# Block-causal self attention on Trainium2: the row maxima are turned one step earlier and their units are dealt out again

## What is computed

```python
scores = jnp.einsum('bhqd,bhkd->bhqk', q, kh) / jnp.sqrt(jnp.float32(D))
scores = jnp.where(allowed_pos[None, None], scores, NEG)
scores = jnp.where(causal[None, None], -jnp.inf, scores)
p = jax.nn.softmax(scores, axis=-1)
out = jnp.einsum('bhqk,bhkd->bhqd', p, vh)
```

## Time and profile before

| what | value |
|---|---|
| median of 3 runs (lowest to highest) | 3237.11 us (3233.18 to 3238.16) |
| the profiled execution's own time | 3233.07 us |
| its span | 3231.4 us |
| busy over the span: TensorE, VectorE, ScalarE, GpSimd | 93%, 55%, 38%, 60% |
| self attention's first score, last sum | 535.0 us, 1153.6 us |

### The profile page before, as it was taken

How to read it: one execution, slowest core, us unless ns; L and a number is a source line. 1 busy time by engine, 2 the same in 40 slices (tenths; PEclk the granted TensorE clock), 3 DMA queues, 4 the chain that set the end, 5 groups by cost and what they waited for, 6 DMA issues and landing times. The chain is left out here.

```text
span 3231.4 us, 39692 instructions
## 1 busy us (share of the span) xinstructions
PE 2997.9 (93%) x15242; PEld 1968.5 (61%) x15242; DVE 1766.7 (55%) x2884; ACT 1225.6 (38%) x2307; POOL 1923.7 (60%) x999
## 2 busy tenths in 40 slices
PE   7999999999999959859999999999959999999999
PEld 6888886444444438734444444444427888888887
DVE  4455657777777547647777777777532222122220
ACT  2212223555555522205666666666632111111111
POOL 3324323888887766526888888888877443333332
PEclk9999999999999979968999999999979999999999
DMA  6555764445555045453424242332042010010100
GB/s 205 173 163 189 233 206 122 109 106 115 118 117 119 17 146 195 170 137 65 87 57 99 57 94 65 72 87 57 11 134 62 27 39 30 23 40 27 40 13 14
DMA packets 199538, 310.17 MB, mean 96 GB/s; under 512 B 15011, under 2 KB 93363, under 8 KB 199347
## 3 DMA queue, kind: packets, MB, share of 16 engines
q1 hardware_dynamic: 199350, 307.64, 34.8%
HBM read 189.04 MB, written 117.44 MB: 95 GB/s over the span
## 5 line engine op out<-in xcount | busy, mean ns | idle before, releaser
L1254 POOL TENSOR_TENSOR e_probs<-e_probs 128x2048 f32<-128x2048 f32 x160 | 731.4, 4579 | 189.1 <-ACT e_probs L1230 184.3
L1230 ACT ACTIVATE e_probs<-e_st 128x512 f32<-128x512 f32 x1024 | 557.4, 598 | 407.8 <-PE e_st L1412 389.9
L1308 DVE TENSOR_REDUCE e_neg_max<-e_nat 128x1 f32<-128x1024 f32 x512 | 602.0, 1217 | 169.3 <-PE e_nat L1395 164.4
L1230 ACT ACTIVATE b_probs<-b_st 128x512 f32<-128x512 f32 (+3 forms) x768 | 340.3, 490 | 279.0 <-PE b_st L1412 268.8
L1305 DVE CUSTOM_DVE_ANT_0 b_nat<-b_nat,mask_qk 128x128 f32<-128x128 f32 (+7 forms) x512 | 374.4, 785 | 80.9 <-PE b_nat L1395 79.5
L1412 PE MATMUL e_st<-e_qs,e_ks 98*128 98x512 f32 x1024 | 395.3, 430 | 10.0 <-DMA e_qs<-e_max_lo 6.8
L1715 POOL TENSOR_TENSOR m_hid_lo<-m_hid,m_hid_hi 128x512 fp32r<-128x512 f32 x128 | 168.3, 1315 | 390.5 <-DVE m_hid_hi L1752 390.5
L1254 POOL TENSOR_TENSOR b_probs<-b_probs 128x1536 f32<-128x1536 f32 (+3 forms) x128 | 374.7, 2927 | 38.1 <-PE b_pv L1424 35.2
L1395 PE MATMUL e_nat<-e_ks,e_qs 96*128 96x512 f32 x1024 | 345.8, 422 | 40.1 <-DMA e_vs<-cv 25.4
L1752 DVE CAST m_hid_hi<-m_hid 128x512 fp32r<-128x512 f32 x128 | 58.5, 457 | 570.6 <-ACT m_hid L1631 570.6
L1412 PEld LDWEIGHTS e_st<-e_qs,e_ks 98*128 98x128 f32 x1024 | 175.7, 189 | 263.5 <-ACT e_probs L1230 195.9
(11 more groups left out here) (180 smaller groups left out, 5165.3 us busy)
## 6 DMA issues: line engine op xcount, KB each, us to landing
b_qs<-sq_hi SPq DMA_DIRECT2D x32, 512.0 KB, 6.8
b_ks<-sk_hi SPq DMA_DIRECT2D x32, 512.0 KB, 11.2
e_qs<-cq_hi SPq DMA_DIRECT2D x32, 512.0 KB, 6.8
e_ks<-ck_hi SPq DMA_DIRECT2D x32, 512.0 KB, 14.6
ck_hi<-p_part_hi SPq DMA_DIRECT2D x32, 256.0 KB, 3.2
ck_lo<-p_part_lo SPq DMA_DIRECT2D x32, 256.0 KB, 3.6
cv<-p_tok_out SPq DMA_DIRECT2D x32, 256.0 KB, 3.0
p_x<-in_x SPq DMA_DIRECT2D x8, 1024.0 KB, 7.4
```

The lines of the kernel that those rows point to most:

```text
L1230: act.activation(probs[:, home(n, k), j, first:TOK], st_ps[:, bank_at("scores", blk), first:TOK], ACT.Exp).then_inc(exped, 1)
L1254: pool.tensor_tensor(into, into, probs[:, home(n, k), :, first:TOK], ALU.add).then_inc(added, 1)
L1308: dve.tensor_reduce(neg_max[:, u:u + 1], found, AX.XY, ALU.max, negate=True).then_inc(maxed, 1)
```

## The change

One line. In the causal attention the turn moves from step NS - 3 = 9 to step NS - 4 = 8, and on TensorE from head 2 (there in front of `weigh`) to head 3 (behind it). The cross attention keeps its numbers. Since `START` is worked out from `TURN`, the planner deals the units anew.

```diff
--- before.py
+++ after.py
@@ -1037,7 +1037,7 @@
     last_step = {h: max(n for n, st in enumerate(steps) if st[0] == h) for h in range(HALVES)}
     NS, NBLOCKS = len(steps), len(steps) * HG
     UNITS = HG * KT
-    TURN, TURN_HEAD, PE_TURN_HEAD, TURN_BANK = NS - 3, 2, 2 if causal else 3, 2
+    TURN, TURN_HEAD, PE_TURN_HEAD, TURN_BANK = NS - (4 if causal else 3), 2, 3, 2
```

## The result

| | before | changed |
|---|---|---|
| median, lowest to highest | 3235.14 us (3231.02 to 3238.16), 4 runs | 3252.65 us (3251.03 to 3254.57), 4 runs |
| span of the profiled execution | 3231.4 us | 3249.3 us |
| self attention's first score, last sum | 535.0, 1153.6 us | 540.2, 1170.7 us |

The changed kernel takes 1.0053 times as long (95% interval 1.0037 to 1.0069): slower by 17.5 us. The prediction was 3252, which was 15.5 us above the 3237.11 of the kernel before; taken beside the changed kernel, that kernel has 3235.14.

The account below looks back on a forecast made before the run. TensorE was the likely bound, with GpSimd's chain 0.12 us behind from A to B. Fourteen rounds at +0.95 us gave +13.3, the start +2.2: +15.5 on 3237.1, so 3252 us, range 3234 to 3261 for 8 in 10.

Parts of the forecast that it names:

- The floor of A to B: GpSimd's work from clear 8 to clear 0 keeps A to B at 15.86 us or more, against 15.98 before.
- A to B: On TensorE, from the last score of step 8 to weigh of step 0 in the next set; 15.98 us before.
- the chain: GpSimd's gapless work beside A to B, start of clear 8 to start of clear 0: 13.93 us, 13.87 at the end.
- The rival without a floor: Clear 0 reaches weigh 0 sooner, so the whole saving in A to B counts: 3235 us; chance 0.16.
- B to A: On TensorE, from weigh of step 0 to the next last score of step 8: 22.07 us before, 23.14 foretold.
- columns + waits: The two terms of B to A: units' columns +0.17 us and waits for banks +0.90 us a set.
- unit 2 in step 6: On TensorE it waits for bank 2, which unit 7 holds: 1.05 us, with the extra 1.15.
- The rival by which VectorE runs further ahead: The waits of steps 5 to 7 don't come, a set takes 37.25 us, the whole 3228; chance 0.12.
- The rounds: 14 rounds from set 0 to set 14, each 39.0 us in place of 38.05: +13.3 us.
- The start: Three more units are made ahead of set 0, beside the projections; its last score of step 8 comes 2.2 us late.
- The end: From set 14 to set 15 the old kernel is already at the floor; set 14's missing units give nothing.
- The clock: Rival: new waits before weigh 11 and weigh 0 lower the granted clock, some 4 us a set, 3310; chance 0.03.

Follow-up runs that it names:

- e3: The changed kernel with GpSimd's normalise of the first half moved from between clear 9 and clear 10 to in front of clear 1 of the next set; 3241.36 us.
- e1: The kernel before with only the turn on TensorE moved from head 2 to head 3 of step 9, behind weigh, units unmoved; 3254.14 us.
- e6: The changed kernel with the planner told that step 3 has 1.5 us more room, so units move there; 3242.83 us.
- e2: The changed kernel with the turn in step 8 at head 2, in front of weigh, instead of head 3; 3254.32 us.
- e11: e10 without the planner edit of e6, so with the changed kernel's own units; 3247.13 us.
- e4: The kernel before with the same move of normalise as in e3; 3233.86 us, ratio 0.9996.
- e10: e9 with the first half's store between two parts of the loads, four ahead and three behind; 3215.89 us, ratio 0.9947.
- e5: The changed kernel with the first half's normalise put off to step 3 of the next set, in front of clear 3; 3262.10 us.
- e8: e5 with the store of the first half behind all loads of the set after next; 3368.69 us, ratio 1.0423.
- e9: e8 with the units of e6; 3318.25 us, ratio 1.0276.

## Why the prediction was right

*The floor of A to B.* Foretold 15.86, measured 15.87 in 14 sets. It was worked out from set 14 to 15 of before, where TensorE already stood still for the chain. That clear 0, and not the exponentials that the row of `weigh` 0 names, releases B is shown by e3: with 1.28 us less on GpSimd alone, B comes 1.24 earlier. The rival without a floor is refuted. The prediction has no price for a third road, that of the rows. For the change it needed none: with the turn in step 8 no score waits for them. The three rounds of before that wait for the rows, and e1, show that this road, too, had no slack to speak of.

*B to A, step by step* (set 7; a step is counted from the last score of the step before it, so the first starts at 812.83 before and at 823.24 now):

| step | before | now | measured | foretold: columns + waits |
|---|---|---|---|---|
| 4 | 1.97 | 2.23 | +0.26 | +0.25 + 0 |
| 5 | 4.07 | 3.48 | -0.59 | -0.19 - 0.31 |
| 6 | 4.09 | 4.41 | +0.32 | -0.11 + 0.41 |
| 7 | 4.25 | 5.68 | +1.43 | +0.58 + 0.79 |
| 4 to 7 | 14.38 | 15.80 | +1.42 | +1.42 |

"Foretold" splits the two terms of the prediction by step with its own prices of the units. (With these prices the columns add up to 4.70 and 4.87 us, not to the 4.68 and 4.85 that it wrote; the difference of 0.17 is the same.) With steps 2 and 3, which lose units, the whole is 22.06 to 23.15, +1.09, against the +1.07 forecast. Single waits: unit 2 in step 6 is issued 1.30 behind the score in front of it, 1.07 above the 0.235 of a matmul of 512 (1.15 foretold). In step 7 unit 6 comes 0.80 behind its score, 0.57 above it (0.65), and unit 7 comes 0.91 behind unit 6, whose two matmuls of 448 account for some 0.42 (0.49 against 0.47). The rival by which VectorE runs further ahead is refuted; a set would have become shorter only with under 2.00 us of waits in steps 5 to 7. That their length was a matter of order is shown by e6, which takes some of them away.

*The rounds.* 14 times from A to A: 533.4 became 546.4, +13.0 (+13.3 foretold). Each round grew by 0.98 from the usual 38.05, a little more than the 0.95 foretold, but before has a first round of 38.12 and three of 38.2 to 38.3, those in which the first score waits for the rows.

*The start.* A of set 0 was to come 2.2 late. It comes 5.34 late, but 2.60 of that is there at the first turn of the self attention (528.15 before, 530.75 now), ahead of anything that the change touches. What is left is 2.74. The term was 0.5 too low: I had set 0 gaining more from its missing units than it did. The 2.60 has no term in the prediction. Its cause stays open, but it looks like the scatter of single executions: in e2 to e11 the first turn comes at anything from 521.6 to 531.6 us, and between 264 and 480 us the traces of before and changed differ by 5.8, ahead of all that the change touches.

*The end.* Set 15 was to cost nothing and is 1.2 us shorter (from B to the last sum 43.9 before, 42.7 now). The terms so add up to +2.7 +13.0 -1.2 = +14.5 at the last sum, against +15.5; the last sum is in fact 17.1 later, 2.6 of which are those from ahead of the stage. Between the medians the difference is 17.5 us, 2.0 more than the sum foretold. So that 3252 was met to within 1 us is luck: the 2.0 is made up for by the base, 3237.1 in the prediction and 3235.14 beside the changed kernel. In the profiled executions, 17.1 us apart at the last sum, the terms account for 14.5.

*The clock.* In the changed kernel it did not fall, though the waits in front of `weigh` 11 and `weigh` 0 came as foretold (0.30 and 0.97). But my ground against it, that the old waits of 1.0 and 0.5 had done no harm, was weak: e1 has waits of that size some steps away and falls in four sets.

*Against the name of the thing.* The change takes away 1.5 us of waits on TensorE in each set and wins 0.12, since GpSimd stood 0.12 behind. For this it pays 1.09 in a part of the set that had no slack at all, because the number that places the turn also places the units.

## What to carry to other kernels

Before a wait of 1 us is taken away, find the second road that ends at the same place, and how far behind it stands: here 0.12 us, read off the gap between the end of one GpSimd instruction and the start of the `weigh` that needs it. There can be more than two, as the rows of e1 show. A number that moves two things wants to be tried with each alone; here the turn in step 8 cost nothing and the deal of the units cost 1.1 us a round. The parts of a possible gain showed none against the kernel before until all were there (e4: the same; e6: 0.3% slower; e10: 0.5% faster). And when an instruction is put off, follow it through each queue behind it: in e5 the loads and in e8 the store behind `normalise` cost more than GpSimd had gained.

## What the runs showed of the hardware that was not expected

- The granted clock can fall to half behind waits of TensorE of under 1 us, in some passes of a loop and not in others: in e1 in four of 14 sets, 5 us each, behind waits of 0.34 and then 0.73 to 1.68 us, while ten sets with waits of 0.34 and 0.73 to 1.76 us kept the full clock. In e6, five short stretches cost 1.4 to 2.8 us each. The changed kernel, with waits of 0.30 and 0.97 in each set, had none. What tells the passes apart stays open.
- A store of 256 KB issued behind a batch of loads on the same queue lands when they have: the first half's store takes 11.5 us in the median behind all seven loads (e8), 4.0 behind four of them (e10), and 2.0 in front of them (before). In e8 and e9, VectorE and TensorE wait for it.
- GpSimd's chain is steady: clear 8 to clear 0 was 13.91 to 13.94 in all 14 full sets of the changed kernel, and without one instruction of 1.28 it was 12.70 in e3, 1.22 less.
